# The first attention's written order of work: 31 instead of 23 first-pass units ahead, units placed group by group

## The reference, cut to what matters

```
x: 2 x 1024 x 128, 16 heads of 8
q, k, v = x_heads @ Wq.T, @ Wk.T, @ Wv.T
scores  = einsum('bqhd,bkhd->bhqk', q, k) / 128**0.5      # no mask
attn    = softmax(scores, axis=-1)
Y       = einsum('bhqk,bkhd->bqhd', attn, v)
out     = Y @ Wo.T + bo
```

## Time and profile before

| | us |
|---|---|
| median of 3 runs | 992.84 |
| lowest, highest | 990.77, 993.43 |
| the profiled execution | 993.59 |
| its span, first to last instruction | 991.8 |

### The profile page before, as it was taken

One profiled execution on the slowest core, in us unless ns is written; L12 is line 12 of the kernel. 1 busy time (PEld: TensorE's weight loads), 2 busy tenths in 40 slices (PEclk: granted clock), 3 DMA queues, 4 the chain that ended last, 5 costly groups with the idle time before them and its releaser, 6 DMA issues. The chain is left out here.

```text
span 991.8 us, 22162 instructions
## 1 busy us (share of the span) xinstructions
PE 873.3 (88%) x8501; PEld 448.1 (45%) x8501; DVE 803.1 (81%) x1600; ACT 606.5 (61%) x1312; POOL 200.2 (20%) x249
## 2 busy tenths in 40 slices
PE   5689999999999998893779999999998988786888
PEld 3312222222222222892434545554546666565578
DVE  7798999999999990555689888889864777799687
ACT  3318888888888887452416777777772447232652
POOL 2301132521312120451110011102010031233132
PEclk9659999999999999896859999999998998988899
DMA  2541535454156421111364674345301000000001
GB/s 72 167 127 46 140 79 123 91 107 97 47 121 144 124 61 22 48 34 56 68 195 119 170 155 97 82 99 112 74 8 36 1 1 1 1 1 0 4 7 37
DMA packets 61782, 73.72 MB, mean 74 GB/s; under 512 B 20247, under 2 KB 45968, under 8 KB 61662
## 3 DMA queue, kind: packets, MB, share of 16 engines
q1 hardware_dynamic: 47354, 49.22, 20.7%
q0 software_dynamic: 8576, 17.86, 7.4%
q10 hardware_dynamic: 5748, 5.22, 1.6%
HBM read 44.59 MB, written 18.16 MB: 63 GB/s over the span
## 5 line engine op out<-in xcount | busy, mean ns | idle before, releaser
L1035 DVE TENSOR_REDUCE a_negmax<-a_mbank 128x1 f32<-128x1024 f32 (+4 forms) x640 | 491.4, 819 | 40.5 <-PE a_mbank L828 18.7
L990 ACT ACTIVATE a_probs<-a_ebank 128x512 f32<-128x512 f32 (+3 forms) x896 | 426.3, 559 | 104.3 <-PE a_ebank L856 52.3
L828 PE MATMUL a_mbank<-a_moving,a_still 48*128 48x512 bf16 (+4 forms) x1280 | 274.7, 377 | 23.2 <-DVE a_ident L997 14.1
L856 PE MATMUL a_ebank<-b_moving,b_still 50*128 50x512 bf16 (+4 forms) x1280 | 249.5, 356 | 9.6 <-ACT a_probs L990 7.3
L881 PE MATMUL a_acc<-a_probs,a_slot_v 128*32 128x512 f32 (+3 forms) x1792 | 216.8, 560 | 0.8 <-ACT a_probs L990 0.7
L856 PEld LDWEIGHTS a_ebank<-b_moving,b_still 58*64 58x64 bf16 (+1 forms) x1280 | 83.1, 101 | 200.9 <-ACT a_probs L990 167.2
L828 PEld LDWEIGHTS a_mbank<-a_moving,a_still 56*64 56x64 bf16 (+1 forms) x1280 | 70.1, 102 | 122.4 <-DVE a_negmax L1035 94.0
L865 PE MATMUL a_ebank<-a_bias_b,anti 64*64 64x176 bf16 (+4 forms) x1728 | 77.9, 226 | 0.0
L865 PEld LDWEIGHTS a_ebank<-a_bias_b,anti 64*64 64x64 bf16 x1728 | 64.7, 107 | 4.7
L836 PE MATMUL a_mbank<-bias_a,anti 64*64 64x176 bf16 (+2 forms) x576 | 66.2, 236 | 0.0
L881 PEld LDWEIGHTS a_acc<-a_probs,a_slot_v 128*32 128x32 f32 x1792 | 36.4, 108 | 53.6 <-issue 36.1
(11 more groups left out here) (389 smaller groups left out, 1114.0 us busy)
## 6 DMA issues: line engine op xcount, KB each, us to landing
a_slot_v<-vo SPq DMA_DIRECT2D x16, 512.0 KB
b_moving<-stack SPq DMA_DIRECT2D x64, 96.0 KB
b_still<-stack SPq DMA_DIRECT2D x32, 192.0 KB
a_still<-stack SPq DMA_DIRECT2D x60, 96.0 KB, 2.9
a_moving<-stack SPq DMA_DIRECT2D x60, 96.0 KB, 3.0
expert<-in_expert_rows POOLq DMA_DIRECT2D x8, 578.0 KB, 4.1
a_bias_b<-trow SPq DMA_DIRECT2D x32, 66.0 KB
stack<-expert SPq DMA_DIRECT2D x4, 384.0 KB, 2.8
```

The lines of the kernel that those rows point to most:

```text
L828: last = nc.tensor.matmul(mbank[COLS * c:COLS * (c + 1), bank, lo - left:hi - left], S.a_still[rows, q % 2, pr, at[c]:at[c] + COLS], S.a_m ...
L856: last = nc.tensor.matmul(ebank[COLS * c:COLS * (c + 1), step % NE, lo:512], S.b_still[rows, buf, pr, at:at + COLS], S.b_moving[rows, buf, ...
L990: nc.scalar.activation(probs[:, (q * G + g) % NPB, j, lows[g]:512], ebank[:, step % NE, lows[g]:512], ACT.Exp).then_inc(p_full, 1)
L1035: nc.vector.tensor_reduce(to[:, at:at + 1], mbank[:, (index - 1) % NM, 0:right - left], AX.X, ALU.max, negate=True).then_inc(m_empty, 1)
```

## The change

Three lines of the written order of the first attention are replaced. No instruction is added or removed and `AHEAD` stays 23. Quad 0's words hold 40 units (32 before), those of quads 1 to 6 hold 32 each, and those of quad 7 hold 1 (9 before), so that 31 of the next quad's 32 units are issued when a second pass begins.

```diff
     False: [
-        "01u23u 01u2V3u 01u2V3u 01u2V3u 01u2V3u 01u2V3Bu 01u2V3u 01u2V3u "
-        "01u2V3u 01u2V3u 01u2V3u 01u2V3u 01u2V3u 01u2V3Au 01u2V3u 01u2V3u",
-        "01u2V3u 01u2V3u 01u2V3u 01u2V3u 01u2V3u 01u2V3Bu 01u2V3u 01u2V3u "
-        "01u2V3u 01u2V3u 01u2V3u 01u2V3u 01u2V3u 01u2V3Au 01u2V3u 01u2V3u",
-        "01u2V3u 01u2V3u 01u2V3u 01u2V3u 01u2V3 01Bp2V3 01p2V3 01p2V3 "
-        "01p2V3 01p2V3 01p2V3 01p2V3 01p2V3 012V3 012V3 012V3V",
+        "0u12u3 u0u123 uu01u2uVuu3 Vu0uVuBu123 u01u23 u0V1uu2V3 0u1u2V3 01uu2V3 "
+        "01uu2V3 uu012V3 uu012V3 uA0u12V3 0uu12V3 01uu2V3 0u1u2V3 uu012V3u",
+        "01u2V3 u01u2V3 u01u2V3 u01u2V3 u01u2V3 uB0u12V3 u0u12V3 u01u2V3 "
+        "u01u2Vu3 01u2V3 u01u2V3 u01u2V3 0u1u2VA3 u01u2V3 u01u2V3 u01u2Vu3",
+        "012V3 012u3 V012V3 0123 V012VB3 01p23 V01p2V3 01p23 "
+        "V01p2V3 01p23 V01p2V3 01p23 V01p2V3 0123 V012V3 0123VV",
     ],
```

## The result

| | us |
|---|---|
| the changed kernel, median of 4 runs | 1011.62 (1007.59 to 1014.07) |
| the kernel before, median of 4 runs in all | 993.13 (990.77 to 996.62) |
| ratio | 1.0179, 95% interval 1.0129 to 1.0229 |
| profiled execution after, its span | 1007.59, 1005.8 |

The change makes the kernel slower by 18 us, which is clear of the noise. The forecast was +7, range 993.5 to 1004.5: the direction was right, the size was not, and the time lies above the range.

The account below looks back on a forecast made before the run. The prediction took a loop of waits of 2.39 us a word as the bound, VectorE only until quad 0's words; 8.3 + 1.1 - 2.4 = +7.0 us gave 1000.6 beside 993.59, hence a 999.9 us median, range 993.5 to 1004.5.

Parts of the forecast that it names:

- What else is moved: Unit DMAs, GpSimd's steps and the later stage: shifts costed at nothing; a late load would be 1 to 2 us a quad.
- a rival for late loads: Moved loads come late in each of six quads, 1 to 2 us each, 1006 to 1012 us; chance 0.04.
- Quad 0: 8 more units where VectorE was already the bound: +8.3 us, bounds 7.5 and 12.
- VectorE's gaps: Quad 0's first words: VectorE may starve at the first V, taken as 0.7 us, between nothing and 1.61.
- The rival that TensorE stays at 1.2 GHz for longer: Quad 0: first three products all take 1.94 us and VectorE starves, +3.5 us, 1003.4 us; chance 0.08.
- Quads 1 to 6: Most words keep the 2.39 us loop; moved turnings and units add 0.19 us a quad, +1.1 us, bounds -2 and +5.
- Quad 7: Fewer units save nothing; the new V pattern and B's shorter wait save 2.4 us, bounds -1 and -6.9.
- Pairs with a `p`: Quad 7's four word pairs with a p: the second V stalls near 0.37 us, saving 0.06 us in each.
- The loop of waits: Plain words: waits among exponential, score 2, V and the next 3 set 2.39 us a word, with or without units.
- VectorE is the bound, and the new order keeps it fed: Half quads fall from 20.11 to 19.1 us, 13 of them saving 13 us, 986 us; chance 0.11.

Follow-up runs that it names:

- e1: Changed kernel with GpSimd's clearing transfer of sorted_rows issued 8 units later, behind SP's loads; median 1002.59 us, ratio to before 1.0098.
- e4: Changed kernel with the clearing 8 units later and quad 0's 40 units spread evenly; median 1002.02 us, ratio to before 1.0095.
- e9: Kernel before with 40 units spread evenly in quad 0, 1 in quad 7, and the clearing later; median 1006.70 us, ratio 1.0134.
- e7: Kernel before with only the turnings A and B moved, three words changed in each of quads 0 to 6; median 987.70 us, ratio 0.9962.
- e8: Kernel before with the turnings moved and quad 7 rewritten from word 5, projections in words without V; median 985.94 us, ratio 0.9923.
- e10: Changed kernel, unchanged, profiled once more; that execution took 1010.95 us.
- e3: Changed kernel run again, unchanged, as yardstick; median 1014.48 us, ratio to before 1.0229.
- e11: Changed kernel, unchanged, profiled a further time; that execution took 1011.98 us.
- e6: Changed kernel with the clearing 8 units later and GpSimd's division of batch 0 behind expert 4's load; median 1002.00 us, ratio 1.0090.
- e5: Kernel before with the clearing issued ahead of gather(1), so ahead of quad 3's rows of maxima; median 1000.66 us, ratio 1.0082.
- e2: Kernel before with the clearing set 7 units earlier, issued after the rows and half of the operands; median 992.76 us, ratio 0.9989.

## Why the prediction was wrong

**The failed step** is "What else is moved": "GpSimd's steps wait for unit numbers; since quad 0 is longer by as much as the units are earlier in the order, their times stay. [...] I cost these at nothing". Their times did stay (the clearing at 191.72 us for 192.79). What moved was everything else against them. Quad 3's rows of maxima went out at 193.06 instead of 187.3 us, because the order up to that place was 10 us longer and `A` only one word earlier. So the clearing passed them. That cost 6.5 us, with the loop's rule intact everywhere else; without it (e1) the median is 1002.59. The same step missed that GpSimd's multiplication would meet the cast: 1.3 to 2.9 us. I had a rival for late loads (0.04), but put it on SP's issue and on all six quads; it was one place, the neighbour was another engine's transfer, and what held the new order were the 4 KB rows, of which the prediction said nothing.

**Quad 0** was mis-sized: 8.3 forecast, 10.2 to 11.2 measured in the six profiles with the change's quad 0, 10.1 and 11.0 with the even ones of e4 and e9. Word 5's last exponential was forecast 94.5 us with the start of the kernel before and came at 95.44, with a start 1.5 us earlier. VectorE's gaps were 2 x 1.60 instead of 0.7. The rival that TensorE stays at 1.2 GHz for longer (0.08) was right in kind. Its "against", that TensorE is kept full, did not hold (busy 3.71 and 3.63 of 4 us in the two stretches from 70 to 78 us). The clock rose 28.9 to 30.5 us behind L954 for 23.6, and then it fell again, which the rival did not have. In e4 and e9 it rose at 25.8 and 26.0 us and stayed. The Trainium skill, page TensorE: Matmul & The Clock Gate, section Part 1: The HAM clock gate, says that the engine is throttled by default and that activity releases it. The rise agrees (it came behind 4.00 us busy of 4.00); the fall came behind 3.21 of 4.00. I should have asked this of the stretches where the change thins TensorE's work, not only of the first rise. How little of the time hangs on it stands under e4.

**Quads 1 to 6** were to cost 0.19 us each and gained 0.18. Read word by word, `B` costs 2.52 - 2.39 = 0.13 now (0.28 forecast) and `A` 0.04 (0.25 forecast). ScalarE takes `A`'s copy while it waits for the `3` anyway, which I had overlooked. A `u` between `V` and `3` costs 0.25 (0.22 forecast), a `u` ahead of `1` nothing (0.08). e7 turns the places of the turnings into a gain.

**Quad 7** gained 1.5 and not 2.4. Pairs without a `p` take 4.42 us, as worked out (4.78 - 0.36). Pairs with a `p` in the word of two products take 4.93, where I had 4.72. e8 shows that the place of the `p` was the reason.

**What held.** The loop of waits sets 2.39 us whether units are there or not: plain words were 2.39 before, after and in all experiments (but for the three words of e9's quad 3), and e9's quad 7 was unchanged without its units. The rival "VectorE is the bound, and the new order keeps it fed" is refuted by the same rows, and with it the reading that the Trainium skill, page Perfetto Trace Analysis, section Identifying the Most-Contended Engine, would give. The eight units cost what VectorE needs for them, 8 x 1.18 = 9.4 us, and 0.7 to 1.8 us more, which no run splits further.

## What to carry to other kernels

Before moving work to where an engine is idle, look whether the engine that feeds it has room there; here eight reductions were moved from a stretch whose pace was set by a loop of waits, and where they cost nothing, to one in which VectorE was full. When a stream that others are timed by is reordered, list for each large transfer what is issued within its landing time on either side, and how long the small urgent ones can wait: 4 KB behind 1495 KB cost 6.5 us. Take the loop of waits apart instruction by instruction; a turning of maxima put where its engines wait anyway went from 0.43 us to 0.04, but to 0.10 when the same word stood in the old order (e7).

## What the runs showed of the hardware that was not expected

- A VectorE cast of 128 x 16 took 1.86 to 2.12 us instead of 0.17 while GpSimd ran a TENSOR_TENSOR of 128 x 1024 (after, e1, e4, e10), and both ended together. Where the cast started no later than that instruction (e3, e11) it took 0.17, and the VectorE subtraction of 128 x 16 behind it took 2.28 and 2.22 and ended with it. In e6, where they did not meet, both took 0.17 to 0.18. The reductions out of PSUM beside the same instruction kept their 1.22 us.
- Transfers of 4 KB issued 1.3 us behind one of 1495 KB held the score that needs them until about when that one landed (the score started at 205.60 us and the clearing landed at 206.34; in e5 198.97 and 198.76), though they came from another engine's queue. Their own landing is not recorded. Those issued 2.7 us ahead of it (e2) were in time.
- The granted clock fell from 1.00 to 0.5 in the midst of matmul work, with TensorE busy 3.21 of 4 us in the stretch before, and took until 94.7 us to come back. It did so in all six profiles with this quad 0.
